# Householder tridiagonalization on one core: waits, operation order and the cutting of the side work in each reflection

## The reference

```
# layer 0: eight Euler steps
h = jnp.einsum('bnd,ed->bne', x, fc_in_w) + fc_in_b
def euler_step(h, _):
    ax = jnp.einsum('nm,bmd->bnd', adj_mx, h)
    f = alph * 0.5 * (ax - h) + h @ w_eff - h + x0
    return (h + dt * f, None)
...
# layer 1: spectral convolution
L_norm = d_inv_sqrt[:, None] * L * d_inv_sqrt[None, :]
_, U = jnp.linalg.eigh(L_norm)
agg = jnp.einsum('mn,bnd->bmd', U.T, features)
h = jax.nn.relu(agg @ W1 + b1)
return jnp.einsum('nm,bmd->bnd', U, h @ W2 + b2)
```

## Time and profile before

| | |
|---|---|
| median of three runs | 4877.47 us (4869.52 to 4891.39) |
| the profiled execution | 4896.3 us (span 4894.5) |
| busy, share of the span | PE 69%, DVE 65%, ACT 21%, POOL 16% |
| instructions | 71,887 |
| mean granted TensorE clock | 0.766 |
| the reflections | 95 to 2537 us |

### The profile page before, as it was taken

One profiled execution on the slowest core, in us unless ns is written; L12 is line 12 of the kernel. 1 busy time (PEld: TensorE's weight loads), 2 busy tenths in 40 slices (PEclk: granted clock), 3 DMA queues, 4 the chain that ended last, 5 costly groups with the idle time before them and its releaser, 6 DMA issues.

```text
span 4894.5 us, 71887 instructions
## 1 busy us (share of the span) xinstructions
PE 3372.1 (69%) x20820; PEld 2043.9 (42%) x20820; DVE 3161.2 (65%) x17005; ACT 1017.9 (21%) x3735; POOL 761.4 (16%) x3360
## 2 busy tenths in 40 slices
PE   3899999899889989999970000000065857599998
PEld 2676565655565565655540000000043623244433
DVE  6657788787878877778787889999922122202333
ACT  0212222222222222222210000000012122314542
POOL 1111122222212222222222221111000000000000
PEclk7657999699879968878785555555587978689998
DMA  2000000000000000000000000000000000000000
GB/s 87 2 1 2 2 2 2 2 2 2 2 2 2 2 1 2 1 1 1 1 1 0 0 0 0 0 0 0 0 0 0 17 0 0 0 0 0 0 0 34
DMA packets 3105, 21.15 MB, mean 4 GB/s; under 512 B 432, under 2 KB 560, under 8 KB 1072
## 3 DMA queue, kind: packets, MB, share of 16 engines
q1 hardware_dynamic: 2736, 16.85, 0.9%
HBM read 12.66 MB, written 4.19 MB: 3 GB/s over the span
## 4 chain that ended last, share of the span: by engine, by line
DVE 49%; PE 42%; issue 5%; ACT 2%; POOL 1%; DVEq 1%; DMA 0%; SPq 0%; POOLq 0%; ACTq 0%
PE ps L906 6%; PE ps L624 5%; DVE H L1711 5%; PE ps L576 3%; PE ps L913 2%; DVE XYEG L1459 2%; PE ps L618 2%; DVE jq L1329 2%; DVE C L1484 2%; DVE H L1329 2%; DVE tsc L1471 2%; DVE SO L1496 2%; PE ps L661 2%; DVE tsc L1481 2%; ACT H L1092 2%
## 5 line engine op out<-in xcount | busy, mean ns | idle before, releaser
L624 PE MATMUL ps<-C 128*32 128x131 f32 (+39 forms) x10200 | 418.6, 301 | 0.0
L632 PEld LDWEIGHTS ps<-XYEG 128*128 128x128 f32 x1020 | 191.6, 224 | 380.0 <-DVE XYEG L1459 341.4
L967 POOL TENSOR_SCALAR step<-XYEG,tsc 128x8 f32<-128x8 f32 (+3 forms) x510 | 152.7, 299 | 1267.8 <-DVE tsc L1469 1267.8
L1157 ACT ACTIVATE tsc<-tsc 128x1 f32<-128x1 f32 x510 | 103.5, 203 | 1139.4 <-DVE tsc L1449 1139.4
L576 PE MATMUL ps<-C,LT 128*128 128x512 f32 x512 | 318.4, 707 | 0.0
L576 PE MATMUL ps<-WK,LT 128*128 128x512 f32 x512 | 316.0, 702 | 0.0
L1171 ACT ACTIVATE sz<-C,tsc 128x4 f32<-128x4 f32 (+3 forms) x510 | 151.7, 297 | 736.0 <-POOL C L968 736.0
L906 PE MATMUL ps<-C,V 128*128 128x512 f32 (+1 forms) x504 | 287.5, 727 | 8.5 <-issue 7.5
L618 PE MATMUL ps<-C,XYEG 128*128 128x1 f32 x1020 | 221.3, 286 | 104.1 <-DVE C L1484 83.0
L624 PEld LDWEIGHTS ps<-C 128*32 128x32 f32 x10200 | 281.8, 124 | 16.5
L645 PEld LDWEIGHTS ps<-C,XYEG 128*128 128x128 f32 x958 | 181.2, 223 | 224.1 <-POOL C L968 165.6
(11 more groups left out here) (473 smaller groups left out, 7608.3 us busy)
## 6 DMA issues: line engine op xcount, KB each, us to landing
out_x<-X SPq DMA_DIRECT2D x4, 1024.0 KB, 3.9
X<-in_x SPq DMA_DIRECT2D x2, 1280.0 KB, 20.6
X<-in_x SPq DMA_DIRECT2D x1, 1536.0 KB, 16.9
...
```

Source lines behind the costliest of these rows:

```text
L624: m = mm(ps[q * QUAD:(q + 1) * QUAD, 0, 0:c + n], SI[:, b, 0, 2 * j:2 * j + 1].broadcast_to([P, QUAD]), AS[:, b, q, k * QUAD:P + n], start ...
L632: mm(ps[:, 1, 1:3], spread(XYEG[:, r % 2], k, 2), XYEG[:, r % 2, k, 1:4:2], start=True, stop=True).then_inc(S["pivot_ps"], 1)
L967: step(g_.tensor_scalar(step2[:, k:KB, :], this[:, :, 2:4], tsc[:, 7:8], None, ALU.mult))
```

## The change

In `reflect`, the waits of DVE are spread so that each operation has at most one: xm_ready goes to L1450's place, the wait for `saved` goes away, since the scalars now alternate between the halves of a tile PQ. ACT keeps scalars and vector one reflection later, behind the next root (`keep`). Beta and its partner come from one scalar_tensor_tensor on pairs (sign times x1 and sign; norm and zero), both reciprocals from the next operation, and a new product gives the two factors by which the coefficients are formed. The pivot element x1 is multiplied out behind the row products, no longer ahead of them, and y's pivot element comes from the ones-product of a second reduction. With one block left the pivot column is computed inside the next reflection. The diagonal's factor is applied to the whole row after the loop. At three places two waits change their order: POOL's L967, ACT's L1171, `pivot_column`.

The pieces of layer 0 are cut in two. Gaps hold 2 and 2 halves in the first two quarters, 2 and 1 in the third, 1 and 1 in the last, and each panel update gets three further gaps of 1 to 4 halves. The idle product has 256 columns in place of 512. The plan now ends at reflection 465. The pieces themselves hold 1482 halves for 761 pieces.

```diff
-HEAT = ((512, 512),) * KB
+IDLE = 256
+ROOM = ((2, 2), (2, 2), (2, 1), (1, 1))
+PANEL_ROOM = ((1, 2, 4), (1, 2, 3), (1, 1, 1), (1, 1, 1))
...
                 pe.wait_ge(S["x_ready"], r)
-                pe.wait_ge(S["e_ready"], r)
-                mm(ps[:, 0, c + n:c + n + 1], spread(XYEG[:, r % 2], k, 2), SI[:, k, 0, 2 * j:2 * j + 1],
-                   start=True, stop=True, skip_group_check=True)
-                if r > 1:
-                    pe.wait_ge(S["zu_ready"], r - 1)
                 for b in range(k, KB):
...
                 m.then_inc(S["row_ps"], 1)
+                mm(ps[:, 1, 0:1], spread(XYEG[:, r % 2], k, 2), SI[:, k, 0, 2 * j:2 * j + 1],
+                   start=True, stop=True).then_inc(S["coef_ps"], 1)
                 pause(r, 0)
 
-                pe.wait_ge(S["y_ready"], r)
-                pe.wait_ge(S["g_ready"], r)
-                mm(ps[:, 1, 1:3], spread(XYEG[:, r % 2], k, 2), XYEG[:, r % 2, k, 1:4:2], start=True, stop=True).then_inc(S["pivot_ps"], 1)
                 pe.wait_ge(S["dots_in"], r)
-                mm(ps[:, 3, 0:1], ones[:], dots[:], start=True, stop=True).then_inc(S["dots_ps"], 1)
+                mm(ps[:, 3, 0:2], ones[:], dots[:], start=True, stop=True).then_inc(S["dots_ps"], 1)
+                mm(ps[:, 1, 1:2], spread(XYEG[:, r % 2], k, 2), XYEG[:, r % 2, k, 3:4], start=True, stop=True).then_inc(S["pivot_ps"], 1)
                 pause(r, 1)
...
-                pool.wait_ge(S["beta_ready"], r)
                 pool.wait_ge(S["g_ready"], r)
+                pool.wait_ge(S["beta_ready"], r)
...
+                act.wait_ge(S["scale_ready"], r)
                 act.wait_ge(S["zu_ready"], r)
-                act.wait_ge(S["scale_ready"], r)
...
+                if near:
+                    pivot_column(r, True)
+                dve.wait_ge(S["coef_ps"], r)
+                m_sg = ch.mark(ts_(sg, x1, 0.0, -0.5, ALU.is_lt, ALU.add))
...
+                m_sgx = ch.mark(tt(sgx, x1, sg, ALU.mult))
...
+                    go(ttr(jk[:, 0, k:KB], x, y, dots[:, 0:1]))
+                    m = ttr(jk[:, 1, k:KB], e, y, dots[:, 1:2])
...
-                if r > 1:
-                    dve.wait_ge(S["saved"], r - 1)
                 ch.need(m_c1)
-                tt(mu, c1, sg, ALU.mult).then_inc(S["beta_ready"], 1)
+                stt(pair, tsc[:, 3:5], c1, tsc[:, 0:2], ALU.mult, ALU.subtract).then_inc(S["beta_ready"], 1)
                 dve.wait_ge(S["beta_ready"], r)
-                m_un = ch.mark(stt(un, x1, mu, mu, ALU.subtract, ALU.mult))
-                ch.need(m_un)
-                v.reciprocal(tsc[:, 8:10], tsc[:, 6:8]).then_inc(S["scale_ready"], 1)
+                v.reciprocal(own, pair).then_inc(S["scale_ready"], 1)
+                dve.wait_ge(S["scale_ready"], r)
+                go(tt(tsc[:, 14:16], own, ns.broadcast_to([P, 2]), ALU.mult))
...
-                if r > 1:
-                    dve.wait_ge(S["so_done"], r - 1)
-                dve.wait_ge(S["g_ps"], pivots(r))
+                if not known:
+                    dve.wait_ge(S["g_ps"], pivots(r))
+                    if r > 1:
+                        dve.wait_ge(S["so_done"], r - 1)
```

More of the change, by code:

```diff
@@ L100, in pivots, with pauses @@
     return r - r // PANEL
+def pauses():
+    for p in range(PANELS):
+        for r in panel_rows(p):
+            yield (r, 0), r + 1, ROOM[r // P][0]
+            yield (r, 1), r + 1, ROOM[r // P][1]
+        if p < PANELS - 1:
+            r, k = (p + 1) * PANEL, (p + 1) * PANEL // P
+            for h in range(3):
+                yield (r, 2 + h), r, PANEL_ROOM[k][h]
 class Gaps:
     def __init__(self):
-        self.tensor, self.scalar, self.pool = {}, {r: [] for r in range(REFLECTIONS + 2)}, {r: [] for r in range(REFLECTIONS + 2)}
-        self.gap, self.seen = 0, {}
+        self.slots = [(at, root) for at, root, room in pauses() for _ in range(room)]
+        self.tensor, self.scalar, self.pool = {}, {r: [] for r in range(REFLECTIONS + 4)}, {r: [] for r in range(REFLECTIONS + 4)}
+        self.next, self.seen = 0, {}
     def at(self, key, r):
@@ L120, in unit @@
         for part, needs in enumerate(parts):
-            g = max([self.gap] + [2 * self.seen[n] - 1 for n in needs])
-            self.tensor[g] = key + (part,)
-            self.gap = g + 1
-        return self.at(key, g // 2 + 2)
+            after = max([0] + [self.seen[n] for n in needs])
+            while self.slots[self.next][0] < (after, 1) or after > 0 and self.slots[self.next][0][0] == after and self.slots[self.next][0][1] > 1:
+                self.next += 1
+            at, root = self.slots[self.next]
+            self.tensor.setdefault(at, []).append(key + (part,))
+            self.next += 1
+        return self.at(key, root)
 def plan_gaps():
@@ L137, in plan_gaps @@
     for u in range(EULER + 1):
-        p.unit(("w", u), [[last]] * KB)
+        p.unit(("w", u), [[last]] * (2 * KB if u > 0 else KB))
         last = ("w", u)
@@ L533, in out_part, with w_part @@
                         m.then_inc(S["table_ps"], 1)
-            def w_part(u, nb):
+            def w_part(u, part):
                 k = EULER - u
+                nb, half = (part, 1) if u == 0 else (part // 2, part % 2)
                 if u == 0:
@@ L584, in pause @@
             def pause(r, h):
[L586 to L600 removed]
+                pieces = PLAN.tensor.get((r, h), [])
+                if len(pieces) == 0 and r > EULER_END:
+                    pe.wait_ge(S["eu_sb"], 4 * TILES)
+                    keep_clock(IDLE)
+                for kind, i, part in pieces:
+                    if kind == "table":
+                        table_part(i, part)
+                    elif kind == "out":
+                        out_part(part)
+                    elif kind == "w":
+                        w_part(i, part)
+                    else:
+                        tile_part(i, part)
             pe.wait_ge(S["lt_ready"], 1)
@@ L1156, in reflect @@
                 act.wait_ge(S["norm_ready"], r)
-                fn(tsc[:, 1:2], tsc[:, 2:3], ACT.Sqrt).then_inc(S["root_ready"], 1)
+                fn(tsc[:, 2:3], tsc[:, 0:1], ACT.Sqrt).then_inc(S["root_ready"], 1)
+                if j > 0 and r > 1:
+                    keep(r - 1)
                 for kind, i in PLAN.scalar[r]:
```

157 lines of the change are left out of this document (85 added, 72 removed).

## The result

The changed kernel takes 4693.37 us (median of 4 runs, 4666.7 to 4715.6) where the kernel before, run beside it, takes 4884.43 (4869.52 to 4901.56): a ratio of 0.9605, with an interval of 0.9544 to 0.9666. Its profiled execution took 4695.6 us, 200.7 less than that of before. It is faster by 4%, inside the range, but 48 us behind the forecast: 32 of them are missing in the sum (-201 for -233), and the other 16 come from the step from the profiled execution to the median, for which 19 us had been taken off.

The account below looks back on a forecast made before the run. PE was taken to bound reflections at 1.2 GHz, the chain through DVE those at 2.4 GHz. Chain, low-clock and update gains, less 2 us behind the loop, sum to -233 from 4896.3: 4663, median 4645 us, range 4560 to 4770.

Parts of the forecast that it names:

- rival 1: Last quarter: the lighter PE loses the clock and may sit at 1.2 GHz throughout; 4743 us, chance 0.18.
- The chain of the last quarter: Last quarter at full clock: a reflection takes about 2.97 us for 3.52, -0.55, as 2.31 to the store plus 0.65.
- The largest term: PE begins the row products at once, without the x1 product ahead of them: 0.31 us a reflection at full clock.
- The chain of the other quarters: Reflections of the first three quarters at full clock get shorter by 0.17, 0.14 and 0.17 us.
- beta +0.19: Third quarter: beta, where the side chain to SO starts, comes 0.19 us later in a reflection.
- +0.1 because the x1 product, two pieces and the pivot product now queue: First quarter, where PE ends last: these products queue behind each other on PE, about 0.1 us more a reflection.
- The turned waits: POOL's L967, ACT's L1171 and the pivot column, with two waits in changed order: +0.07 us each.
- The last quarter at low clock: Last quarter: 30 slow reflections go from 5.49 us to 3.3, midway between both clocks: 65 us less.
- Work in updates: Half pieces in the panel updates: between +15 and -30 us, taken as -8; beyond this they may hold the clock.
- the second: Rival: the clock holds everywhere, a third of the first two quarters' low-clock time going at full clock; 4577 us, chance 0.12.
- The third: Rival: more, smaller PE steps and a later first piece keep the first two quarters at 1.2 GHz; up to 5070 us, chance 0.07.
- the fourth: Rival: moved waits stay double elsewhere, stalls reappear at `scaled`, the clock stays as it is; 4850 us, chance 0.05.

Follow-up runs that it names:

- e1: The changed kernel with two half pieces in each gap of the last quarter and a 512-column idle product there: 4588.07 us, ratio 0.9376 to the kernel before.
- after: The changed kernel itself, with the whole change, against the kernel before: 4693.37 us, ratio 0.9605.
- e6: e5 with the x1 product ahead of the row products again, as it stood before the change: 4655.51 us, ratio 0.9498 to the kernel before.
- e2: The changed kernel with the two waits at POOL, ACT and the pivot column back in the old order: 4652.09 us, ratio 0.9489 to the kernel before.
- e5: The changed kernel with e2's old wait order and e3's full side work together: 4542.05 us, ratio 0.9269 to the kernel before.
- e8: e5 with two and one halves in the last quarter's gaps and idle products of 512 and 256 columns: 4559.31 us, ratio 0.9301 to the kernel before.
- e4: e3 without half pieces or idle product in the panel updates: 4634.41 us, ratio 0.9466 to the kernel before.
- e9: e5 with a second wait, on a semaphore long over, put ahead of beta and of the column's store: 4557.95 us, ratio 0.93 to the kernel before.
- e3: The changed kernel with two halves in each gap of all quarters and a 512-column idle product in the reflections: 4574.41 us, ratio 0.9346 to the kernel before.
- e10: e5 with the last quarter's pivot column behind SO again, as in the other quarters: 4532.15 us, ratio 0.9234 to the kernel before.

## Why the prediction was right, and where not

**The sign** was right, with a chain that is shorter and a clock that holds better in the middle quarters (0.90 for 0.82 and 0.83). **The size**, -201 us for -233, is near by luck: the first three quarters gained 74 us more than the sum gave them and the last 100 less. The measured 4693 lies in the interval of the forecast (4595 to 4700), but in the last quarter it was rival 1 that happened.

**The chain of the last quarter** was right to 0.06 us: 2.91 us in e1 (2.87 in after's two fast reflections) for 2.97. The largest term, the x1 product behind the rows, is shown by e6.

**The chain of the other quarters** was sized too small: 0.17, 0.14 and 0.17 us were predicted, 0.38, 0.32 and 0.32 measured (4.51 to 4.13, 4.15 to 3.83, 3.84 to 3.52). The failed term is "beta +0.19" in the third quarter and "+0.1 because the x1 product, two pieces and the pivot product now queue" in the first. The second reduction follows the first by 0.07 us (1492.06 to 1492.13 in after), where I had put a whole 0.16. Sign times x1, put at 0.10, costs next to nothing: from the reduction of y (L1504 at 1491.76) to that of the sum (1492.06) it is 0.30 us with it, and 0.31 before without it (1632.48 to 1632.79). And beta's second wait is gone. So in reflections that aren't slow beta is at most 0.02 us later by medians, not 0.19, and the side chain that starts at beta comes 0.17 sooner than the sum had it: that is what is missing in 0.14 and 0.17. In the first quarter the queue on PE did not bind: the rows start 2.85 us into the reflection, 3.22 before (medians of those that aren't slow). That is 0.37, the 0.31 of x1 and a store that comes sooner, with nothing of my +0.1.

**The turned waits** cost what the sum put on them (0.07 each; measured 0.08, 0.06, 0.11). They stood on the path in the second and third quarter (0.18 us a reflection, e2), and e2 and e5 show that this part of the change should not have been made.

**The last quarter at low clock** is the step that failed: "if it no longer falls at the update, the 30 slow reflections of each late quarter run at 2.97". Two reflections into the quarter it fell, to 0.52 in the mean, and a reflection took 3.81 us. By the prediction's own words it is wrong if the fourth stretch falls instead of rising to 0.9. It had named this as rival 1 with a chance of 0.18, and had set against it that with a shorter chain the same gap is relatively less idle. Between e1 and after it costs 2.3%, some 110 us. Rival 1's price was 79, by 3.6 us a reflection; it was 3.81, for a half holds PE 0.99 and not 0.93 us, and the other products take 1.87 instead of 5.49 - 2 x 1.87 = 1.75. The time (4693) still lies under its 4743, since the first three quarters gained more. The Trainium skill (TensorE: Matmul & The Clock Gate, "What's actually happening") has the low level as the default that activity lifts; e1 and after agree, with 0.98 and 0.52 in the same quarter, and so does the fall in e8 where two reflections have no side work.

**Work in updates**: "-8" for their own length. They became 12, 12 and 5 us shorter in the first three quarters and 7 longer in the last, at the low clock: 22. Its value for the clock was 60 us (e4), and what I had hoped of it, the third quarter at 0.9 or more, came: 0.90.

**Of the rivals**, the second (first quarters recover) came true in part: 14 slow reflections fewer in the second quarter, 19 us by the table; in the first all 39 are there still. The third did not show at all, the first quarter is 41 us shorter. Of the fourth a part: in the first three quarters `scaled` is now what DVE waits for. L1543 starts 0.48, 0.47 and 0.44 us behind the store by medians, 0.21 where nothing holds it, so 0.23 to 0.27 late; the turned orders are 0.11 of that (0.37, 0.35 and 0.33 in e5). That is about the 0.2 us that the prediction set as a sign of being wrong, yet the chain gained more than the sum said. At the store a second wait costs nothing, its waits being over; at beta it costs 0.07 us (e9). The Trainium skill (VectorE: DVE Perf Modes, "The DRAIN you can't avoid"), by which a semaphore after each of eight copies cost nothing, agrees with the first and not with the second.

**Open** is why e4, without work in the updates, still holds 0.90 in the last quarter where before had 0.84, and why e2's third quarter ran at 0.85. Open as well is how much the hole at the plan's end costs. Single quarters of kernels with the same code there differ by up to 0.04 in the clock (after and e1 in the third, 0.90 and 0.86) and by up to 20 us (first quarter: after 703, e3 683), so a difference of less than that in one quarter shows nothing, and the ratios decide.

## What to carry over

Filler work and spare work on TensorE is not free to thin out: before halving it, ask what the granted clock is in the stretch that has less, and compare a kernel with less of it against one with more: here the shorter chain brought nothing where the clock was halved (3.81 us a reflection, 3.55 before). Look for stretches where a plan leaves no filler at all, even of two or three steps. Put products that nobody waits for behind those on the chain, even a single column, and where an instruction has two waits, write the one that ends last first in the code. Split such a change into chain, filler and wait order and time each, since here chain and full side work brought 6.5% together (e3), the thinned side work took 2.6% of it back (after), and the turned waits had cost another 0.8%.

## What the chip showed beyond what I expected

- The order in which two waits of one instruction are written matters: with the late one second 0.18, 0.09 and 0.15 us on POOL, ACT and DVE, with the late one first 0.10, 0.03 and 0.04. A second wait is free where both are over (e9, the store).
- TensorE sat at 1.2 GHz for all but 14 of 494 us with a busy share of 99% (after), and at 2.4 GHz with the same 99% (e1): the busy share does not tell the two apart. What differs is the side work, one half in each gap against two.
- In six kernels with the new chain and full gaps in the last quarter (e1, e3, e5, e6, e9, e10) the clock fell there once, and each time where the plan's end leaves two to three reflections without side work. With three quarters of the work the same hole cost 130 us at 1.2 GHz, while reflections before and behind it with the same work ran at 2.4 GHz (e8).
- A reduction by the custom instruction follows another by 0.07 to 0.08 us, where I had counted 0.16 for each from the pivot column's.
